# The products and sums of a feed-forward weight on GpSimd instead of VectorE, with newly planned engine orders, in a transformer layer on eight cores

## The chip, the cores and the metric

One Trainium2 chip (trn2), eight cores, one program on all of them; each core computes one of the eight batch elements. The time is the device time in microseconds of the slowest core. The engines of a core are TensorE (PE in the rows, PEld for its weight loads), VectorE (DVE), ScalarE (ACT), GpSimd (POOL) and SyncE (SP). Each executes its own instructions in a fixed order and waits on semaphores; transfers run beside them.

## The reference

For each batch element x is 2048 x 1024 in fp32, with 16 heads of width 64:

```python
x = x + attention(layernorm(x)) @ Wo + bo      # Q, K, V from Wq, Wk, Wv; scores / 8 + mask; softmax
# mask(i, j): -inf for j > i, 0 for j == i, -0.25 * log(i - j) for j < i
x = x + ffn(layernorm(x))
# ffn: complex product of the halves of x with W_real, W_imag (512 x 512 each), plus bias
W = einsum('abcd,cefg->abefdg', G1, G2).reshape(512, 512)     # c = 4 terms; once real, once imaginary
```

So each of the two feed-forward matrices is a sum of four outer products of small factors, and the kernel needs them as one 1024 x 1024 bf16 weight (real, imaginary, and minus imaginary, each where it belongs).

## The kernel before

**Stages.** The queries come in four chunks (c) of 512 rows. Each has 8 pairs of heads (p), and for each pair the keys come in tiles of 128 (mt, 4c + 4 of them). One (c, p, mt) is a step; there are 320, numbered g. A step is: two score matmuls on TensorE into stP (lines 1118 and 1120), an exp on ScalarE over both heads into PT (line 996), a product with the decay factors on VectorE (line 857), and twelve matmuls of 32 columns width for pv and for the denominators pr (lines 1142 and 1148). After a pair's last step ScalarE takes the reciprocal of pr by Ln and Exp (1004, 1006) and VectorE writes attnT (874).

Between the steps TensorE runs groups, each a matmul chain into one of two banks gp: T (transposes of the normalised xnrot, line 1044), K, Q (1057), V (1067), N and B (norm bounds for the exp's bias, 1078 and 1083), O (output projection, 1093), F (feed-forward, 1103). Each group is evicted by VectorE or ScalarE; some evictions of K, Q and T go to whichever the planner picks.

**The feed-forward weight.** It is built in 8 units (real and imaginary, four row tiles each) of 7 steps: a product of broadcast slices of g1s and g2s into wacc, then three times a product into wtmp and a sum wacc + wtmp. All are 128 x 512 fp32 (`wf_step`, lines 785 to 807, on VectorE). Each step waits for the one before by the semaphore s_wf. After step 7 of a unit ScalarE rounds wacc into two places of Wf (`wf_round`, lines 971 to 978); the next unit's first step waits for both by s_wfr. The factors g1s and g2s are the last transfers of GpSimd's first batch (lines 653 and 655). All eight units have to be done before attnT of chunk 2 is written (line 863, since wacc lies in its memory), before V of the last tile and before the first F group.

**What sets the order.** `make_fill` deals the groups out between the steps; this isn't touched. `make_orders` then lists all work as tasks with an engine, a length in us and predecessors, and simulates the engines: on ScalarE and VectorE it takes, of the tasks that are ready, the one with the earliest latest time. Its result, ACT_ORDER, DVE_ORDER and PE_ORDER, is emitted as it stands. Key lines of it are the tasks of the exp ("X", line 280), of the decay product ("P", 282), of the weight steps ("W", 316) and of the roundings ("WR", 318), and the lag after each task (lines 338 and 409):

```python
task("act", ("X", g), 0.19 + 0.00088 * w, ("S", g), ...)
task("dve", ("P", g), 0.03 + 0.00063 * w, ("X", g), ...)
task("dve", ("W", i), 0.6, ("W", i - 1) if i else ("dma", "g"), ...)
```

GpSimd's own program is short: an iota, the first batch of loads, then from line 659 on a wait for the last K group, the load of Wo, and the transfers that add bo and bfn.

Of the kernel before, what the change touches and what calls it, by code (L numbers as in the profile page):

```python
# [29 lines left out]
PATIENCE = (0.1, 0.15, 0.2, 0.3)  # L30
ROUNDS = 4
# [184 lines left out]
def make_orders(plan):  # L216
# [21 lines left out]
    for k in pe:  # L238
# [8 lines left out]
        else:  # L247
# [9 lines left out]
            if k1 == PASSES[what]:  # L257
# [41 lines left out]
    for i, (c, p) in enumerate(pairs):  # L299
        n = c * 4 + p // 2 - 2  # L300
        task("dve", ("SQ", c, p), 0.75, ("E", ("K", c, p)), ("E", ("Q", c, p)), i and ("SQ",) + pairs[i - 1],
             n >= 0 and ("D", ("N", n // 4, n % 4)))
    for c in range(NCH):
        for h in range(2):
            before = (c, 0) if h else (c - 1, 1) if c else None
            task("dve", ("BD", c, h), 0.15, ("E", ("N", c, 2 * h)), ("E", ("N", c, 2 * h + 1)), before and ("BL",) + before)
            task("act", ("BL", c, h), 0.3, ("BD", c, h), c and ("D", ("B", c - 1, h)))
            task("dve", ("BM", c, h), 0.12, ("BL", c, h), before and ("BM",) + before, c and ("D", ("B", c - 1, h)))
            task("dve", ("BN", c, h), 0.15, ("E", ("B", c, h)), before and ("BN",) + before)
# [17 lines left out]
    def latest(pe_at):  # L327

        late = {}
        for k in tasks:  # L330
            stack = [] if k in pe_at or k in late else [k]
            while stack:
# [4 lines left out]
                else:  # L337
                    late[k] = min([pe_at.get(u, late.get(u)) for u in users[k]] + [1e4]) - tasks[k][1] - 0.12
# [890 lines left out]
```

## Time and profile before

| | us |
|---|---|
| median of 3 runs | 563.18 (561.47 to 565.92) |
| the profiled execution | 561.32 |
| its span, slowest core (7) | 559.8 |
| spans of the eight cores | 555.4 to 559.8 |
| TensorE busy | 517.1 |
| VectorE busy | 461.3 |
| ScalarE busy | 381.9 |
| GpSimd busy | 38.3 |

The span runs from the first to the last instruction of a core, and the time holds what lies around it besides. Busy time is the sum over an engine's instructions; matmuls are pipelined, so a busy TensorE isn't one at its peak. In rows of groups, what stands behind the first bar is busy time in us and the mean of one in ns, and behind the second bar the idle time of the engine just before them with what ended it. A stretch A:B is in us from the span's start.

### The profile page before, as it was taken

Reading aid. Unit: us, or ns where it says so; the run is one execution under the profiler, and the core shown is the slowest. Engines: PE = TensorE matmul, PEld = TensorE weight load, DVE = VectorE, ACT = ScalarE, POOL = GpSimd, SP = SyncE. Lnnn points to the kernel's source line nnn. Section 1 sums busy time; section 2 is a strip of 40 time slices with the busy share of each in tenths; the row PEclk is TensorE's granted clock in tenths of the full one; section 3 lists DMA queues with packets and bytes.
Section 4 is the critical chain, followed back from the end, with each engine's and each line's share of the span. In section 5 each row is a group of like instructions: output and inputs, shape, how many; then the busy total and the mean of one; then the engine's idle time right before and its main releaser. Section 6 shows DMA issues by size and latency. Waiting matters only on the chain.

```text
span 559.8 us, 16753 instructions; the slowest of 8 cores (555.4 to 559.8 us)
## 1 busy us (share of the span) xinstructions
PE 517.1 (92%) x6096; PEld 241.2 (43%) x6096; DVE 461.3 (82%) x830; ACT 381.9 (68%) x526; POOL 38.3 (7%) x51
## 2 busy tenths in 40 slices
PE   1798989899999999989999999999999999999986
PEld 1334444344443444444444444444545444444442
DVE  5645999999999999887777887887888888888683
ACT  3425776778888879866767777777778777786010
POOL 7000000000000000000000020201101011111110
PEclk9999999999999999989999999999999999999999
DMA  8999231000120000010000089756566666457574
GB/s 200 187 170 253 78 114 39 3 2 2 40 78 2 8 34 1 2 47 33 1 3 2 1 121 185 150 137 148 135 152 152 152 151 141 97 130 171 146 153 150
DMA packets 16479, 52.77 MB, mean 94 GB/s; under 512 B 2000, under 2 KB 2000, under 8 KB 15632
## 3 DMA queue, kind: packets, MB, share of 16 engines
q0 software_dynamic: 7328, 28.05, 27.5%
q1 hardware_dynamic: 9072, 23.65, 12.7%
q8 instruction: 52, 0.85, 0.7%
q14 instruction: 27, 0.22, 0.1%
HBM read 51.69 MB, written 8.39 MB: 107 GB/s over the span
## 4 chain that ended last, share of the span: by engine, by line
PE 69%; DVE 9%; ACT 8%; issue 7%; DMA 5%; DVEq 0%; ACTq 0%; POOLq 0%
PE gp L1057 18%; PE stP L1118 11%; PE pv L1142 10%; PE gp L1093 8%; PE gp L1067 8%; PE gp L1103 8%; ACT PT L996 5%; PE pr L1148 4%; DMA Wo<-wo 3%; PE gp L1044 2%; DMA x<-bfn 1%; DVE stat L700 1%; DVE x L773 1%; DVE V L748 1%; DVE attnT L874 1%
## 5 line engine op out<-in xcount | busy, mean ns | idle before, releaser
L996 ACT ACTIVATE PT<-stP,negc 128x1024 bf16<-128x1024 f32 (+1 forms) x320 | 301.4, 983 | 81.8 <-PE stP L1120 80.1
L857 DVE TENSOR_TENSOR PT<-PT,decay 128x1024 bf16<-128x1024 bf16 (+1 forms) x320 | 190.7, 603 | 35.0 <-ACT PT L996 33.2
L1142 PE MATMUL pv<-PT,V 128*32 128x256 bf16 (+3 forms) x2560 | 101.4, 258 | 1.5 <-DVE PT L857 0.5
L1118 PE MATMUL stP<-QT,KT 64*128 64x512 bf16 (+1 forms) x320 | 94.5, 350 | 5.2 <-ACT PT L996 5.0
L1120 PE MATMUL stP<-QT,KT 64*128 64x512 bf16 (+1 forms) x320 | 95.1, 352 | 0.0
L1148 PE MATMUL pr<-PT,ones 128*32 128x256 bf16 (+3 forms) x1280 | 81.2, 257 | 0.7 <-issue 0.7
L1067 PE MATMUL gp<-Wv,xnT 128*128 128x512 bf16 x256 | 67.3, 385 | 8.6 <-DVE V L748 5.0
L1142 PEld LDWEIGHTS pv<-PT,V 128*32 128x32 bf16 x2560 | 56.7, 96 | 38.2 <-issue 35.9
L1057 PE MATMUL gp<-xnT,Wk 128*128 128x512 bf16 x256 | 66.7, 389 | 2.5 <-ACT xnT L968 2.0
L1057 PE MATMUL gp<-xnT,Wq 128*128 128x512 bf16 x256 | 65.0, 380 | 1.0 <-DVE KT L755 0.9
L1093 PE MATMUL gp<-Wo,attnT 128*128 128x512 bf16 x256 | 63.3, 380 | 2.4 <-DVE x L773 1.7
L1103 PE MATMUL gp<-Wf,xn2T 128*128 128x512 bf16 x256 | 63.6, 380 | 2.0 <-DVE outb L782 1.2
L1118 PEld LDWEIGHTS stP<-QT,KT 64*128 64x128 bf16 x320 | 22.6, 93 | 70.4 <-issue 67.3
L874 DVE TENSOR_TENSOR attnT<-pv,recip 64x512 bf16<-64x512 f32 x64 | 44.0, 687 | 4.8 <-ACT recip L1006 3.9
L1067 PEld LDWEIGHTS gp<-Wv,xnT 128*128 128x128 bf16 x256 | 21.6, 99 | 38.5 <-issue 20.7
L1103 PEld LDWEIGHTS gp<-Wf,xn2T 128*128 128x128 bf16 x256 | 22.8, 97 | 34.0 <-issue 11.4
L1057 PEld LDWEIGHTS gp<-xnT,Wq 128*128 128x128 bf16 x256 | 23.1, 98 | 32.3 <-issue 8.7
L1057 PEld LDWEIGHTS gp<-xnT,Wk 128*128 128x128 bf16 x256 | 22.6, 99 | 33.2 <-issue 12.6
L1093 PEld LDWEIGHTS gp<-Wo,attnT 128*128 128x128 bf16 x256 | 22.0, 97 | 34.4 <-issue 13.8
L1044 PE MATMUL gp<-ident_s,xnrot 128*128 128x128 bf16 x256 | 23.3, 233 | 14.3 <-DVE xnrot L710 13.7
L1148 PEld LDWEIGHTS pr<-PT,ones 128*32 128x32 bf16 x1280 | 34.6, 97 | 1.3 <-issue 0.8
L782 DVE TENSOR_TENSOR outb<-gp,x 128x512 f32<-128x512 f32 x32 | 22.1, 690 | 9.9 <-PE gp L1103 9.3
(71 smaller groups left out, 432.1 us busy)
## 6 DMA issues: line engine op xcount, KB each, us to landing
xrot<-x SPq DMA_DIRECT2D x21, 512.0 KB, 4.5
x<-bfn POOLq DMA_DIRECT2D x16, 512.0 KB, 6.4
out<-outb SPq DMA_DIRECT2D x32, 256.0 KB, 3.3
xrot<-bo POOLq DMA_DIRECT2D x12, 512.0 KB, 5.8
xfirst<-x SPq DMA_DIRECT2D x4, 512.0 KB, 6.2
Wk<-wk POOLq DMA_DIRECT2D x2, 1024.0 KB, 21.3
Wq<-wq POOLq DMA_DIRECT2D x2, 1024.0 KB, 27.0
Wv<-wv POOLq DMA_DIRECT2D x2, 1024.0 KB, 32.6
```

The lines of the kernel that those rows point to most:

```text
L857: v.tensor_mul(pt, pt, decay[:, off + no:off + 512].unsqueeze(1).to_broadcast([128, 2, 512 - no])).then_inc(s_pm, 1)
L874: ins = v.tensor_mul(out, pv[x:x + 64, :].rearrange("p (d m q) -> p d m q", d=2, q=64), recip[x:x + 64, :].rearrange("p (m q) -> p m q", q ...
L996: a.activation(p_tile(g, no), st_tile(g, no), AF.Exp, bias=negc[:, c * 8 + p % 2 * 4 + p // 2:][:, 0:1]).then_inc(s_exp, 1)
L1044: ins = t.transpose(ps[:, :].bitcast(BF16)[:, k * 128:(k + 1) * 128], xnrot[:, o + k * 128:o + (k + 1) * 128], ident[:, 0:128])
L1057: ins = t.matmul(ps[:, :], W[:, o:o + 128], xnTv[:, k, :], start=(k == 0), stop=(k == FT - 1))
L1067: ins = t.matmul(ps[:, :], xnTv[:, k, j * 128:(j + 1) * 128], Wv[:, half * 4096 + k * 512:half * 4096 + (k + 1) * 512], start=(k == 0), st ...
L1093: ins = t.matmul(ps[:, :], attnT[:, o + k * 512:o + k * 512 + 128], Wo[:, k * D + ch * 512:k * D + (ch + 1) * 512], start=(k == 0), stop=( ...
L1103: ins = t.matmul(ps[:, :], xn2Tv[:, i % 2, k], Wf[:, k * D + ch * 512:k * D + (ch + 1) * 512], start=(k == 0), stop=(k == FT - 1))
L1118: t.matmul(stP[g % 2][:, no:512], KT[0:64, ks:ks + 128], QT[0:64, qs + no:qs + 512], start=True, stop=True, tile_position=(0, 0))
L1120: t.matmul(stP[g % 2][:, 512 + no:1024], KT[64:128, ks:ks + 128], QT[64:128, qs + no:qs + 512], start=True, stop=True, tile_position=(64, ...
L1142: t.matmul(pv[x:x + 32, half * 256 + no // 2:(half + 1) * 256], V[:, vo + h * 64 + half * 32:vo + h * 64 + half * 32 + 32], p_part(g, h, a ...
L1148: ins = t.matmul(pr[x:x + 32, no // 2:256], ones32[:, :], p_part(g, h, a, no), start=first, stop=last, tile_position=(0, x), skip_group_ch ...
```

## The change

The 56 steps of `wf_step` move word for word from VectorE's program to GpSimd's (the engine `v` becomes `g`). There they stand behind the loads of g1s and g2s and ahead of the wait for the last K group and the load of Wo. In the planner the steps become tasks of no engine with 1.3 us each; the lengths of most other tasks are set anew, mostly shorter, and the lag after a task is 0.18 instead of 0.12 us.

```diff
+LAG = 0.18
...
-                us = {"B": 0.3, "T": 0.65}.get(what, 0.67)
+                us = {"B": 0.25, "K": 0.67, "Q": 0.67}.get(what, 0.61)
...
-        task("act", ("X", g), 0.19 + 0.00088 * w, ("S", g), g and ("X", g - 1), g >= PR and ("V", g - PR),
+        task("act", ("X", g), 0.14 + 0.000853 * w, ("S", g), g and ("X", g - 1), g >= PR and ("V", g - PR),
...
-        task("dve", ("P", g), 0.03 + 0.00063 * w, ("X", g), ("P", g - 1) if g else ("M", 3))
+        task("dve", ("P", g), 0.068 + 0.00052 * w, ("X", g), ("P", g - 1) if g else ("M", 3))
...
-        task("dve", ("W", i), 0.6, ("W", i - 1) if i else ("dma", "g"), i >= 7 and i % 7 == 0 and ("WR", i // 7 - 1), i == 0 and ("M", 2))
+        task("dma", ("W", i), 1.3, ("W", i - 1) if i else ("dma", "g"), i >= 7 and i % 7 == 0 and ("WR", i // 7 - 1), i == 0 and ("M", 2))
         if i % 7 == 6:
-            task("act", ("WR", i // 7), 1.4, ("W", i))
+            task("act", ("WR", i // 7), 1.05, ("W", i))
...
-            finish(k, end + 0.12)
+            finish(k, end + LAG)
...
             g.dma_start(out=g2s[:, :].rearrange("p (t n) -> p t n", t=4),
                         in_=dg2.rearrange("(t p) n -> p t n", p=128)).then_inc(s_g, 16)
+
+            def wf_step(n):
+
+                u, k = divmod(n, 7)
...
+                if n == 0:
+                    g.wait_ge(s_g, 32)
+
+                    g.wait_ge(s_mask, 2)
+                else:
+                    g.wait_ge(s_wf, n)
+                if k == 0 and u >= 1:
+                    g.wait_ge(s_wfr, 2 * u)
...
+                    g.tensor_mul(acc3 if k == 0 else tmp3,
...
+                else:
+                    g.tensor_add(wacc[:, :], wacc[:, :], wtmp[:, :]).then_inc(s_wf, 1)
+
+            for n in range(56):
+                wf_step(n)
...
-                elif what == "W":
-                    wf_step(*n)
```

VectorE's order, from the first full-width decay product of the pair that begins with exp 20. Before (L857 decay product, L803 and L807 the weight's product and sum):

```order
L857 TENSOR_TENSOR PT<-PT,decay 128x1024
L803 TENSOR_TENSOR wtmp<-g1s,g2s 128x512
L874 TENSOR_TENSOR attnT<-pv,recip 64x8x64 x2
L764 TENSOR_SCALAR QT<-gp,bq_s 128x512
L857 TENSOR_TENSOR PT<-PT,decay 128x2x384
L820 TENSOR_TENSOR sqb<-QT 128x512
L821 TENSOR_TENSOR sqb<-KT 128x512
L857 TENSOR_TENSOR PT<-PT,decay 128x2x256
L807 TENSOR_TENSOR wacc<-wacc,wtmp 128x512
L693 BN_STATS stat<-xrot 128x6
L857 TENSOR_TENSOR PT<-PT,decay 128x2x128
L803 TENSOR_TENSOR wtmp<-g1s,g2s 128x512
```

VectorE's order at the same place, of the change (L862 is the decay product now, L784 an eviction of K):

```order
L862 TENSOR_TENSOR PT<-PT,decay 128x1024
L784 TENSOR_SCALAR KT<-gp,cols_s 128x512
L879 TENSOR_TENSOR attnT<-pv,recip 64x8x64 x2
L862 TENSOR_TENSOR PT<-PT,decay 128x2x384
L722 BN_STATS stat<-xrot 128x6
L825 TENSOR_TENSOR sqb<-QT 128x512
L826 TENSOR_TENSOR sqb<-KT 128x512
L729 BN_STATS stat<-xrot 128x6
L731 BN_AGGR stat<-stat 128x2
L862 TENSOR_TENSOR PT<-PT,decay 128x2x256
L862 TENSOR_TENSOR PT<-PT,decay 128x2x128
```

The weight's steps are gone from between the decay products; evictions and layer-norm statistics have closed up.

ScalarE's order around the first rounding, which before stands behind exp 29 (L996 exp, L976 and L978 rounding, L1004 and L1006 reciprocal):

```order
L996 ACTIVATE PT<-stP,negc 128x1024
L996 ACTIVATE PT<-stP,negc 128x2x384
L976 ACTIVATE Wf<-wacc 128x512
L978 ACTIVATE Wf<-wacc 128x512
L1004 ACTIVATE recip<-pr 128x256
L1006 ACTIVATE recip<-recip 128x256
```

ScalarE's order around the first and second rounding of the change, behind exp 15 and behind exp 18 (L999 exp, L979 and L981 rounding):

```order
L999 ACTIVATE PT<-stP,negc 128x2x128
L979 ACTIVATE Wf<-wacc 128x512
L981 ACTIVATE Wf<-wacc 128x512
L988 ACTIVATE nrmx<-nrmx,cst 128x2
L961 ACTIVATE bexp<-gp,cst 128x8
L971 ACTIVATE xnT<-gp 128x8x128
L999 ACTIVATE PT<-stP,negc 128x1024
...
L999 ACTIVATE PT<-stP,negc 128x2x256
L979 ACTIVATE Wf<-wacc 128x512
L981 ACTIVATE Wf<-wacc 128x512
L999 ACTIVATE PT<-stP,negc 128x2x128
```

The eight roundings stand behind exps 29, 40, 51, 66, 74, 87, 101 and 110 before, and behind exps 15, 18, 24, 31, 38, 45, 52 and 60 in the change.

GpSimd's order behind its first batch of loads, of the change; before, the load of Wo follows g2s directly:

```order
L655 DMA g1s<-g1t 128x4x256
L657 DMA g2s<-g2t 128x4x128
L678 TENSOR_TENSOR wacc<-g1s,g2s 128x512
L678 TENSOR_TENSOR wtmp<-g1s,g2s 128x512
L682 TENSOR_TENSOR wacc<-wacc,wtmp 128x512
L678 TENSOR_TENSOR wtmp<-g1s,g2s 128x512
...
L682 TENSOR_TENSOR wacc<-wacc,wtmp 128x512
L689 DMA Wo<-wo 128x8x1024
```

All 56 steps stand ahead of the load of Wo.

## Rows read from the trace of the kernel before

**Rows 1.** The page, busy time: us (share of the span) and instructions.

```profile
PE 517.1 (92%) x6096; PEld 241.2 (43%) x6096; DVE 461.3 (82%) x830; ACT 381.9 (68%) x526; POOL 38.3 (7%) x51
```

**Rows 2.** Stretches: length, busy PE, PEld, DVE, ACT, POOL (instructions), clock, DMA share, GB/s.

```profile
80.00:100.00 20.00, 19.18 (x219) 8.82 (x212) 19.32 (x40) 14.96 (x27) 0.00 (x0) 1.00 0.17 54
100.00:120.00 20.00, 17.71 (x221) 7.91 (x221) 19.52 (x37) 14.41 (x24) 0.00 (x0) 1.00 0.01 3
120.00:150.00 30.00, 29.01 (x379) 13.49 (x371) 29.03 (x56) 24.02 (x37) 0.00 (x0) 1.00 0.06 20
150.00:226.00 76.00, 72.99 (x920) 32.81 (x919) 74.68 (x141) 65.14 (x92) 0.00 (x0) 1.00 0.08 23
...
240.00:320.00 80.00, 75.91 (x980) 35.25 (x972) 62.63 (x113) 57.46 (x69) 0.00 (x0) 0.98 0.05 15
320.00:500.00 180.00, 176.65 (x2323) 83.69 (x2321) 150.60 (x259) 138.87 (x173) 21.38 (x25) 1.00 0.64 142
```

**Rows 3.** Tiles wacc and wtmp: count, min/median/max ns, first and last start.

```profile
L807 DVE TENSOR_TENSOR wacc<-wacc,wtmp x24: 680/683/693, 96.4 to 223.1; 128x512 f32<-128x512 f32 x24
L803 DVE TENSOR_TENSOR wacc<-g1s,g2s x8: 674/682/691, 80.7 to 214.6; 128x512 f32<-128x512 f32 x8
L976 ACT ACTIVATE Wf<-wacc x8: 621/630/638, 105.8 to 225.2; 128x512 bf16<-128x512 f32 x8
L978 ACT ACTIVATE Wf<-wacc x8: 614/624/638, 106.3 to 225.7; 128x512 bf16<-128x512 f32 x8
...
L803 DVE TENSOR_TENSOR wtmp<-g1s,g2s x24: 680/682/693, 92.0 to 222.3; 128x512 f32<-128x512 f32 x24
```

**Rows 4.** Tile g2s: its load's issue on GpSimd, and the time to landing.

```profile
L655 POOL DMA_DIRECT2D g2s<-g2t x1: 767/767/767, 12.7 to 12.7; - x1
...
DMA to landing us min/median/max: 44.9/44.9/44.9
```

**Rows 5.** Groups of GpSimd: the iota.

```profile
L639 POOL IOTA B<- 128x2432 f32 x1 | 2.2, 2152 | 0.4 <-POOLq L436 0.4
```

**Rows 6.** The exps (line 996) from 0 to 80 us, and from 0 to 152 us.

```profile
L996 ACT ACTIVATE PT<-stP,negc x16: 468/790/1114, 43.8 to 77.1; 128x1024 bf16<-128x1024 f32 x4, 128x768 bf16<-128x768 f32 x4, 128x512 bf16<-128x512 f32 x4, 128x256 bf16<-128x256 f32 x4
...
L996 ACT ACTIVATE PT<-stP,negc x60: 464/901/1119, 43.8 to 151.5; 128x1024 bf16<-128x1024 f32 x27, 128x768 bf16<-128x768 f32 x11, 128x512 bf16<-128x512 f32 x11, 128x256 bf16<-128x256 f32 x11
```

**Rows 7.** Timeline, 5 to 17 us, xnrot and one DMA issue; then line 710, tile xrot.

```profile
7.63 0.91 DVE L710 TENSOR_SCALAR xnrot<-xfirst,stat 128x1024 bf16<-128x1024 f32 x1 [0.85 <-ACT stat L923]
...
11.51 0.86 DVE L710 TENSOR_SCALAR xnrot<-xfirst,stat 128x1024 bf16<-128x1024 f32 x1
...
12.66 0.77 POOL L655 DMA_DIRECT2D g2s<-g2t  x1
...
12.89 1.06 DVE L710 TENSOR_SCALAR xnrot<-xfirst,stat 128x1024 bf16<-128x1024 f32 x1
...
15.82 0.80 DVE L710 TENSOR_SCALAR xnrot<-xfirst,stat 128x1024 bf16<-128x1024 f32 x1
...
L710 DVE TENSOR_SCALAR xnrot<-xrot,stat x12: 803/806/809, 53.6 to 249.2; 128x1024 bf16<-128x1024 f32 x12
```

**Rows 8.** Line 857 in all, and GpSimd's transfers of bfn.

```profile
L857 DVE TENSOR_TENSOR PT<-PT,decay x320: 265/681/694, 45.0 to 518.1; 128x1024 bf16<-128x1024 bf16 x128, 128x512 bf16<-128x512 bf16 x32
...
L671 POOL DMA_DIRECT2D x<-bfn x16 | 13.6, 851 | 71.3 <-DVE xnrot L710 71.3
```

**Rows 9.** From 80 to 150 us: line 857 as a stretch, squares and xnrot as groups.

```profile
80.00:150.00 70.00, 22.24 (x41) 1.00 0.08 25
...
L820 DVE TENSOR_TENSOR sqb<-QT 128x512 bf16<-128x512 bf16 x8 | 3.4, 420 | 0.0
L821 DVE TENSOR_TENSOR sqb<-KT 128x512 bf16<-128x512 bf16 x8 | 3.3, 418 | 0.0
L710 DVE TENSOR_SCALAR xnrot<-xrot,stat 128x1024 bf16<-128x1024 f32 x2 | 1.6, 806 | 0.0
```

More of the change, by code:

```diff
@@ L300, in make_orders @@
         n = c * 4 + p // 2 - 2
-        task("dve", ("SQ", c, p), 0.75, ("E", ("K", c, p)), ("E", ("Q", c, p)), i and ("SQ",) + pairs[i - 1],
+        task("dve", ("SQ", c, p), 0.67, ("E", ("K", c, p)), ("E", ("Q", c, p)), i and ("SQ",) + pairs[i - 1],
              n >= 0 and ("D", ("N", n // 4, n % 4)))
@@ L305, in make_orders @@
             before = (c, 0) if h else (c - 1, 1) if c else None
[L306 to L309, printed above, removed]
+            task("dve", ("BD", c, h), 0.13, ("E", ("N", c, 2 * h)), ("E", ("N", c, 2 * h + 1)), before and ("BL",) + before)
+            task("act", ("BL", c, h), 0.19, ("BD", c, h), c and ("D", ("B", c - 1, h)))
+            task("dve", ("BM", c, h), 0.08, ("BL", c, h), before and ("BM",) + before, c and ("D", ("B", c - 1, h)))
+            task("dve", ("BN", c, h), 0.08, ("E", ("B", c, h)), before and ("BN",) + before)
     task("dve", ("M", 0), 2.8, ("A", 3))
@@ L337, in latest @@
                 else:
-                    late[k] = min([pe_at.get(u, late.get(u)) for u in users[k]] + [1e4]) - tasks[k][1] - 0.12
+                    late[k] = min([pe_at.get(u, late.get(u)) for u in users[k]] + [1e4]) - tasks[k][1] - LAG
                     stack.pop()
@@ L354, in length @@
         def length(k, engine):
-            return tasks[k][1] + (0.4 if engine == "act" and k[0] == "E" and k[1][0] == "T" else 0.0)
+            more = {"T": 0.31, "K": -0.08, "Q": -0.08}.get(k[1][0], 0.0) if engine == "act" and k[0] == "E" else 0.0
+            return tasks[k][1] + more
         def finish(k, t):
@@ L656, in _ @@
                         in_=dg2.rearrange("(t p) n -> p t n", p=128)).then_inc(s_g, 16)
+            def wf_step(n):
+                u, k = divmod(n, 7)
+                part, t = divmod(u, 4)
+                acc3 = wacc[:, :].rearrange("p (b e) -> p b e", b=32)
+                tmp3 = wtmp[:, :].rearrange("p (b e) -> p b e", b=32)
+                if n == 0:
[5 more added lines that the diff above has]
+                    g.wait_ge(s_wfr, 2 * u)
+                r = (k + 1) // 2
+                if k == 0 or k % 2 == 1:
+                    o1 = t * 256 + part * 128 + r * 32
+                    o2 = t * 128 + part * 64 + r * 16
+                    g.tensor_mul(acc3 if k == 0 else tmp3,
+                                 g1s[:, o1:o1 + 32].unsqueeze(2).to_broadcast([128, 32, 16]),
+                                 g2s[:, o2:o2 + 16].unsqueeze(1).to_broadcast([128, 32, 16])).then_inc(s_wf, 1)
+                else:
+                    g.tensor_add(wacc[:, :], wacc[:, :], wtmp[:, :]).then_inc(s_wf, 1)
+            for n in range(56):
+                wf_step(n)
             g.wait_ge(s_grp, GROUP_AT[("K", NCH - 1, PAIRS - 1)] + 1)
```

33 lines of the change are left out of this document (6 added, 27 removed).

## The prediction

> **What bounds the kernel now.** I read the page's table of busy time first, then the stretches. Over the whole span TensorE is busy 92%, VectorE 82%, ScalarE 68% and GpSimd 7% [rows 1], so TensorE looks like the only bound, and GpSimd like a free place to put work. The reader should not stop there: the table of stretches [rows 2] shows two regimes. From 80 to 226 us VectorE is busy 19.32 of 20, 19.52 of 20, 29.03 of 30 and 74.68 of 76 us, that is 98%, and TensorE 138.9 of 146 us, so it stands idle for 7.1 us (4.9%). From 320 to 500 us VectorE is at 84% and TensorE at 98.1%. So in the first stretch VectorE sets the pace, in the last one TensorE alone does.
>
> What the change takes off VectorE lies exactly in that first stretch: 24 sums of 0.683 us, 24 products into wtmp and 8 into wacc of 0.682 us, 56 steps from 80.7 to 223.8 us [rows 3]. That is 56 x 0.683 = 38.2 us of the engine that is full there. It looks like a gift. What it is worth depends on what GpSimd's version costs and whom it holds up.
>
> **Part 1, the steps leave VectorE.** If nothing came in their place, the stretch could not run better than TensorE allows. At the idle share of 320 to 500 us (1.9%) the 146 us would hold 2.8 us of TensorE idle instead of 7.1, a gain of 4.3 us; all idle gone would be 7.1 us. So the 38 us are worth 4 to 7 us at the most, because TensorE is next in line. I take 4.3.
>
> **Part 2, the chain on GpSimd.** The 56 steps wait for g2s, issued at 12.7 us and landed 44.9 us later [rows 4], so at 57.6 us; before, VectorE came to the first of them only at 80.7. In the old trace GpSimd runs no product or sum. Bounds from rows: the same operation on VectorE took 0.68 us [rows 3]; GpSimd's iota wrote 2,432 columns in 2.15 us [rows 5], 0.885 ns a column, and three passes over 512 columns (two reads and a write) would be an estimate of 1.36 us. The change's own planner puts 1.3 us for a step with its handshake. I take 1.3, near the upper end, since no GpSimd row here is faster per column than the iota. (The Trainium skill, GPSIMD Engine Reference, section 3.1, has a two-input sum of 2,048 fp32 columns at 4,497 ns; an estimate for 512 columns from it is 1.12 us, and no run here shows it yet.)
>
> Seven steps make a unit, then ScalarE rounds it twice (0.63 and 0.62 us, starts 0.5 us apart [rows 3], so 1.2 us with the handshake) before GpSimd may write wacc again: 7 x 1.3 + 1.2 = 10.3 us a unit. Now the order matters. ScalarE executes in a fixed order, and the new one puts the first rounding after exp 15 and the last behind exp 60, where they stood before after exp 29 and exp 110. By the old trace 16 exps had begun by 80 us, the last at 77.1, and 60 by 152 us, the last at 151.5 [rows 6]. From the first rounding (about 79 us) seven units follow: 79 + 7 x 10.3 = 151 us. The chain is as long as the stretch was before. So even with no side effect the stretch from 79 to 151 us gets no shorter than now: a faster VectorE would bring ScalarE earlier to a rounding whose sum isn't there, and behind that rounding wait the exps, and behind those the products with decay and TensorE's pv matmuls. The start has slack (first unit done at 57.6 + 9.1 = 67, wanted at 79), the seven others have none. What remains of part 1's gain is then the share after 151 us, 76 of 146 us: at most 3.0 us of TensorE idle [rows 2]. I take 2.
>
> **Part 3, what the two engines do to each other.** This has no price in the old trace, and the sum hangs on it. The nearest rows: VectorE's xnrot operation took 0.806 us in 12 of 12 cases when GpSimd did nothing, but 0.91, 0.86 and 1.06 us in the three cases that lay beside GpSimd's DMA issues, and 0.80 us once these had ended [rows 7]. So GpSimd can stretch a VectorE operation by 0.05 to 0.25 us even while it only issues transfers. Against it: the product with decay never took over 0.694 us in 320 cases, though GpSimd issued bias transfers beside it, 16 of bfn alone [rows 8]. So which operations collide matters, and the steps now moved read two tensors and write one, which no GpSimd instruction of the old trace does.
>
> From 80 to 150 us the VectorE operations that have two SBUF inputs, or that were seen to stretch, are 41 products with decay, 16 squares and 2 xnrot: 22.2 + 3.4 + 3.3 + 1.6 = 30.5 us in 59 instructions [rows 9]. Low end: no collision, 0 (a gain is excluded here, since part 1 has counted it). Middle: 59 x 0.13 us (mean of 0.10, 0.05 and 0.25) = 7.9 us, less than the 23 x 0.683 = 15.7 us of steps that leave VectorE in the same stretch, so it would vanish. High end: full exclusion, one waits whenever the other runs. Then the chain and these 30.5 us share one line; into the chain's pauses fit 7 x 1.2 us of roundings and 49 x 0.18 us of handshakes (the planner's figure), 17.2 us. The chain grows by 30.5 - 17.2 = 13.3 us if the pauses are used well, by 30.5 if not at all. The same from VectorE's side: a step that holds it for part of 1.3 us instead of 0.683 us of its own work gives nothing back. I take 15, near the lower end of exclusion: the traffic of a step is far heavier than that of a DMA issue, which already stretched operations by up to 0.25 us.
>
> The rule for it: the Trainium skill, SBUF — State Buffer, section "SBUF: two separate sides", says that VectorE and GpSimd share one read and write port pair by an exclusive lock, held for a whole instruction, by VectorE in a two-port mode or with two SBUF inputs (the latter only against a GpSimd operation that reads SBUF). By that rule the stretched xnrot and the unstretched decay product agree with the trace, and the moved steps are of the kind that blocks; it would give the 13 to 31 us above, and its absence 0. No row before shows the read case itself.
>
> **Part 4, the new orders elsewhere.** The planner is fed shorter lengths (a full exp 1.01 instead of 1.09 us, a full product 0.60 instead of 0.68) and more lag. The stretches' contents are the same, only their interleaving differs. Evictions on ScalarE fall from 50 to 44, on an engine that isn't the bound. From 226 us on there is little TensorE idle to win: 4.1 us in 240 to 320, 3.4 in 320 to 500 [rows 2]. Ends -3 to +3, taken as 0. Wo's load now stands behind the chain on GpSimd; it isn't due before about 320 us, when the chain has long ended, so it costs nothing unless the chain doubles.
>
> **Sum.** Execution profiled: 561.3 us (span 559.8). Part 3 +15, late relief -2, order 0: 574.3 us. The median of the three runs is 1.9 us higher (563.2), and single runs spread over 4.5 us, so I say 574.
>
> **Rivals.** (B) Faster: no collision worth the name. Place: 80 to 226 us, VectorE loses its 98%. For it: the decay product's steady 0.68 us beside DMA issues. Against it: the stretched xnrot, and a chain without slack. It gives 561.3 - 4.3 = 557, or 555 with a little from the orders; own range 551 to 560. It decides if a step stays at or under 1.2 us, so that the chain is no longer than the stretch.
> (C) No change: stretches of the middle kind, 7.9 us, are paid by the 15.7 us that left, and the chain paces as before: 562, own range 558 to 566.
> (D) Slower by the chain alone, with VectorE unharmed: if a step takes 1.6 us, each unit is 2.1 us late, and ScalarE waits 7 x 2.1 = 15 us at its roundings: 576. For it: the roundings stand where the plan had them just ready. Against it: the estimate from the iota ends at 1.36.
>
> **How the numbers follow.** A measurement of this kernel tells about 1% from no change. My forecast (A, both engines collide, 567 to 584) gets 0.40, D 0.05, B 0.36, C 0.19. The time is that of the likeliest: 574. The range goes from B's middle to A's upper end, 554 to 583; A's own range stands above. Slower by over 1%: A and D and the edge of C, 0.46. Faster by over 1% (under about 557.5 against the median): some 0.6 of B, 0.23. Within 1%: 0.31.
>
> **What would show it.** Right: GpSimd's steps last 1.3 us and more, with single ones much longer; decay products between 60 and 160 us above 0.694 us, or idle gaps before them that no other engine explains; ScalarE waiting for wacc before Wf; the 60th exp near 165 us instead of 151.5; after the chain VectorE well under 98%. Wrong: decay products all at 0.68 us beside GpSimd's steps (then B or C); steps of about 1.1 us and TensorE idle under 3 us from 80 to 226 us (B); decay products undisturbed and yet a wait for wacc at each rounding (D). A gain or loss mainly after 240 us would say that part 4 was the cause and my account of the stretch beside the point.

## The result: 4.2% slower, and the profile after

The changed kernel takes 589.14 us (median of 5 runs) against 564.64 us for the kernel before beside it: ratio 1.042, 95% interval 1.038 to 1.046. The profiled execution took 585.04 us. Medians here and below are over all runs, while ratios and intervals leave out those in which the cores of a die ran at a lower clock (one of the five, 649.4 us). I had forecast slower, 574 us with 554 to 583 as the range: the sign was right, but the forecast loss of 11 us is less than half of the 24 us measured.

The page of the changed kernel, busy time, and in 40 slices of the span VectorE's busy tenths and TensorE's granted clock:

```profile
PE 509.9 (87%) x6010; PEld 243.2 (42%) x6096; DVE 461.0 (79%) x780; ACT 379.2 (65%) x520; POOL 108.2 (19%) x107
...
DVE  5545999888989787768787687888888888888693
...
PEclk9999898989998999998999999999999999999999
```

VectorE is busy for 461.0 us, as before (461.3, [rows 1]), though 56 operations (38 us) have left it and only six have come (780 against 830; ScalarE has six fewer, 520 against 526). That is the first thing to see: something filled the hole. GpSimd rose by 69.9 us. The clock dips in the 5th, 7th, 9th and 13th slice, where the old page has a 9 in each; the old page has one 8 too, in the 18th slice, as the new one in its 19th.

The tiles wacc and wtmp, their instructions and who waited (answering [rows 3]):

```profile
L682 POOL TENSOR_TENSOR wacc<-wacc,wtmp x24: 1260/1269/1720, 63.3 to 174.2; 128x512 f32<-128x512 f32 x24
L678 POOL TENSOR_TENSOR wacc<-g1s,g2s x8: 1052/1054/1402, 60.9 to 165.8; 128x512 f32<-128x512 f32 x8
L979 ACT ACTIVATE Wf<-wacc x8: 620/628/638, 84.0 to 180.0; 128x512 bf16<-128x512 f32 x8
...
  ACT Wf L981: 38.4, 7
...
  POOL wacc L678: 38.4, 7
  ACT Wf L979: 0.3, 1
...
L678 POOL TENSOR_TENSOR wtmp<-g1s,g2s x24: 1052/1096/1495, 62.1 to 172.7; 128x512 f32<-128x512 f32 x24
```

A sum takes 1.27 us and a product 1.05 to 1.10, against 0.68 us on VectorE. GpSimd waited 38.4 us in seven cases for ScalarE's roundings, ScalarE only 0.3 us for GpSimd. So the chain of steps was next to never what ScalarE waited for.

VectorE's groups from 60 to 180 us, the kernel before first (the columns: busy us, mean ns, idle before):

```profile
L857 DVE TENSOR_TENSOR PT<-PT,decay 128x1024 bf16<-128x1024 bf16 x36 | 24.6, 682 | 0.3 <-ACT PT L996 0.2
L710 DVE TENSOR_SCALAR xnrot<-xrot,stat 128x1024 bf16<-128x1024 f32 x8 | 6.4, 806 | 0.0
L857 DVE TENSOR_TENSOR PT<-PT,decay 128x768 bf16<-128x768 bf16 x11 | 6.0, 550 | 0.1
...
L821 DVE TENSOR_TENSOR sqb<-KT 128x512 bf16<-128x512 bf16 x12 | 5.0, 418 | 0.0
L857 DVE TENSOR_TENSOR PT<-PT,decay 128x512 bf16<-128x512 bf16 x12 | 5.0, 415 | 0.0
L857 DVE TENSOR_TENSOR PT<-PT,decay 128x256 bf16<-128x256 bf16 x12 | 3.3, 277 | 0.0
```

The same groups of the changed kernel:

```profile
L862 DVE TENSOR_TENSOR PT<-PT,decay 128x1024 bf16<-128x1024 bf16 x25 | 21.6, 875 | 2.7 <-ACT PT L999 2.6
...
L739 DVE TENSOR_SCALAR xnrot<-xrot,stat 128x1024 bf16<-128x1024 f32 x8 | 9.1, 1136 | 0.0
L826 DVE TENSOR_TENSOR sqb<-KT 128x512 bf16<-128x512 bf16 x10 | 8.9, 888 | 0.0
L862 DVE TENSOR_TENSOR PT<-PT,decay 128x256 bf16<-128x256 bf16 x10 | 8.4, 844 | 1.0 <-ACT PT L999 1.0
L777 DVE TENSOR_TENSOR V<-gp,bvB 128x512 bf16<-128x512 f32 x11 | 7.6, 690 | 1.0 <-PE gp L1070 0.7
L825 DVE TENSOR_TENSOR sqb<-QT 128x512 bf16<-128x512 bf16 x10 | 7.5, 748 | 1.7 <-ACT QT L955 1.7
L862 DVE TENSOR_TENSOR PT<-PT,decay 128x768 bf16<-128x768 bf16 x9 | 6.8, 757 | 0.7 <-ACT PT L999 0.7
L862 DVE TENSOR_TENSOR PT<-PT,decay 128x512 bf16<-128x512 bf16 x10 | 6.4, 644 | 0.4 <-ACT PT L999 0.4
L722 DVE BATCH_NORM_STATS2 stat<-xrot 128x6 f32<-128x512 f32 x8 | 5.5, 683 | 0.0
```

The decay product of 256 columns went from 277 to 844 ns, that of 1024 columns only from 682 to 875: what is added doesn't grow with the operation's size, so it is a wait inside the operation's record and not a slower transfer of data. Operations with one input from PSUM (V) or a single 512-column SBUF input (bn_stats) keep their 0.69 us. Summed over the groups that grew: 25 x 0.193 + 9 x 0.207 + 10 x 0.229 + 10 x 0.567 + 10 x 0.470 + 10 x 0.328 + 8 x 0.330 = 25.3 us. These groups have 82 instructions, but not all of them grew. The row of line 862 in the same stretch has its median at 693 ns, the old length of a full product, and its longest at 1,754 ns, so some products wait long and many not at all:

```profile
L862 DVE TENSOR_TENSOR PT<-PT,decay x54: 275/693/1754, 65.1 to 179.7; 128x1024 bf16<-128x1024 bf16 x25, 128x512 bf16<-128x512 bf16 x10, 128x256 bf16<-128x256 bf16 x10, 128x768 bf16<-128x768 bf16 x9
```

The stretches from 60 to 180 us of the changed kernel (columns as in [rows 2]):

```profile
60.00:80.00 20.00, 14.58 (x156) 6.49 (x156) 19.53 (x30) 10.19 (x19) 8.29 (x7) 0.91 0.17 58
80.00:100.00 20.00, 16.46 (x146) 7.61 (x146) 18.94 (x32) 13.19 (x28) 9.59 (x8) 0.91 0.22 65
100.00:120.00 20.00, 15.78 (x216) 7.26 (x215) 18.01 (x30) 13.81 (x25) 13.73 (x13) 1.00 0.04 17
120.00:140.00 20.00, 16.86 (x192) 7.55 (x195) 15.80 (x25) 13.42 (x21) 12.86 (x11) 0.91 0.01 2
140.00:160.00 20.00, 15.52 (x182) 6.33 (x173) 19.15 (x22) 12.55 (x18) 15.97 (x13) 0.94 0.00 1
160.00:180.00 20.00, 16.92 (x182) 8.29 (x185) 18.17 (x27) 13.39 (x20) 9.10 (x7) 0.89 0.16 54
```

TensorE is idle for 120 - 96.1 = 23.9 us of these 120. This is core 2, whose trace lacks 86 of the 6,096 matmul records (x6010 on the page), and a missing record looks like idle time. The old trace's core 7 has them all and shows 7.1 us idle, so the fair comparison is with the old trace's core 2, which lacks 87 records:

```profile
60.00:180.00 120.00, 109.55 (x1371) 52.47 (x1388) 116.94 (x225) 94.46 (x150) 0.00 (x0) 1.00 0.12 38
```

There it is 120 - 109.55 = 10.5 us, so 13.4 us more in the change. The granted clock was 1.00 from 60 to 180 us before; a value of 0.91 means that the clock was at its lower level, 1.2 GHz, for 18% of the time, which takes 9% of the columns that could have passed. Summed, (0.09 + 0.09 + 0.09 + 0.06 + 0.11) x 20 = 8.8 us. Together 22.2 us are gone by 180 us. This only says where the time lies, not what caused it.

The exps of the changed kernel from 0 to 178 us, cut as in [rows 6]:

```profile
L999 ACT ACTIVATE PT<-stP,negc x60: 462/900/1115, 44.7 to 175.3; 128x1024 bf16<-128x1024 f32 x27, 128x768 bf16<-128x768 f32 x11, 128x512 bf16<-128x512 f32 x11, 128x256 bf16<-128x256 f32 x11
```

The 60th exp begins at 175.3 us instead of 151.5, 23.8 us late, and the spans differ by 583.5 - 559.8 = 23.7 us. These are the slowest cores, 2 against 7; on core 2 of both traces the exp is 22.8 us late (152.5 before). The loss arises while GpSimd's steps run; what comes behind them adds or wins back little.

### The profile page after: what moved, and what is told of

Its sections match the earlier page's. It is cut to its first block, busy times and chain, and to the rows that moved or that the text cites. A ratio compares the mean times of both kernels' runs of the same rounds, so it can differ in the third digit from the quotient of the medians.

```text
span 583.5 us, 16667 instructions; the slowest of 8 cores (578.7 to 583.5 us)
## 1 busy us (share of the span) xinstructions
PE 509.9 (87%) x6010; PEld 243.2 (42%) x6096; DVE 461.0 (79%) x780; ACT 379.2 (65%) x520; POOL 108.2 (19%) x107
## 4 chain that ended last, share of the span: by engine, by line
PE 55%; DVE 19%; issue 12%; ACT 9%; DMA 4%; DVEq 1%; ACTq 0%; another core or an unknown queue 0%; POOLq 0%
PE gp L1060 14%; PE stP L1121 8%; PE gp L1096 7%; PE pv L1145 7%; ACT PT L999 6%; PE gp L1070 6%; PE gp L1106 6%; DVE PT L862 4%; DMA Wo<-wo 3%; PE pr L1151 3%; DVE attnT L879 2%; DVE stat L729 2%; DVE xnrot L739 2%; PE gp L1047 2%; DVE stat L722 2%
## 5 line engine op out<-in xcount | busy, mean ns | idle before, releaser
L999 ACT ACTIVATE PT<-stP,negc 128x1024 bf16<-128x1024 f32 (+1 forms) x320 | 301.0, 981 | 89.8 <-PE stP L1123 86.7
L862 DVE TENSOR_TENSOR PT<-PT,decay 128x1024 bf16<-128x1024 bf16 (+1 forms) x320 | 204.5, 651 | 58.6 <-ACT PT L999 56.6
L1070 PE MATMUL gp<-Wv,xnT 128*128 128x512 bf16 x232 | 64.4, 401 | 14.4 <-DVE V L777 5.3
L1060 PE MATMUL gp<-xnT,Wk 128*128 128x512 bf16 x239 | 64.5, 398 | 6.0 <-issue 1.8
L1096 PE MATMUL gp<-Wo,attnT 128*128 128x512 bf16 x237 | 59.0, 380 | 7.8 <-DVE x L802 2.1
L1060 PE MATMUL gp<-xnT,Wq 128*128 128x512 bf16 x247 | 63.0, 385 | 2.7 <-DVE KT L784 1.7
L1106 PE MATMUL gp<-Wf,xn2T 128*128 128x512 bf16 x239 | 59.4, 380 | 4.2 <-issue 2.1
L1121 PEld LDWEIGHTS stP<-QT,KT 64*128 64x128 bf16 x320 | 22.2, 94 | 70.1 <-issue 67.4
L1047 PE MATMUL gp<-ident_s,xnrot 128*128 128x128 bf16 x256 | 23.8, 235 | 16.5 <-DVE xnrot L739 13.9
L682 POOL TENSOR_TENSOR wacc<-wacc,wtmp 128x512 f32<-128x512 f32 x24 | 32.7, 1361 | 3.4
```

Source lines behind the costliest of these rows:

```text
L862: v.tensor_mul(pt, pt, decay[:, off + no:off + 512].unsqueeze(1).to_broadcast([128, 2, 512 - no])).then_inc(s_pm, 1)
L999: a.activation(p_tile(g, no), st_tile(g, no), AF.Exp, bias=negc[:, c * 8 + p % 2 * 4 + p // 2:][:, 0:1]).then_inc(s_exp, 1)
L1047: ins = t.transpose(ps[:, :].bitcast(BF16)[:, k * 128:(k + 1) * 128], xnrot[:, o + k * 128:o + (k + 1) * 128], ident[:, 0:128])
L1060: ins = t.matmul(ps[:, :], W[:, o:o + 128], xnTv[:, k, :], start=(k == 0), stop=(k == FT - 1))
L1070: ins = t.matmul(ps[:, :], xnTv[:, k, j * 128:(j + 1) * 128], Wv[:, half * 4096 + k * 512:half * 4096 + (k + 1) * 512], start=(k == 0), st ...
L1096: ins = t.matmul(ps[:, :], attnT[:, o + k * 512:o + k * 512 + 128], Wo[:, k * D + ch * 512:k * D + (ch + 1) * 512], start=(k == 0), stop=( ...
```

## The experiments

All ratios are against the kernel before, run beside the experiment.

### One part at a time

**move_only**: the steps in GpSimd's program (added lines), with all orders of the kernel before.

```diff
+            for n in range(56):
+                wf_step(n)
...
-                elif what == "W":
-                    wf_step(*n)
```

> The 56 steps go to GpSimd as in the change, but every order (VectorE's without the steps, ScalarE's, TensorE's) stays that of the kernel before, so the roundings stand behind exps 29 to 110. Theory 1 (GpSimd's steps hold up VectorE's operations with two SBUF inputs): nearly the whole loss stays, ratio 1.03 to 1.045 against the kernel before; VectorE's decay products between 60 and 180 us have durations up to 1.7 us. Theory 2 (the newly planned orders lose the time, by the early roundings or otherwise): ratio 0.99 to 1.01. Theory 3 (a chain that ScalarE waits for at its roundings): the roundings come late here, so at most 1.01.

Measured: 590.08 us, ratio 1.0447 (1.0394 to 1.0501). Moving the steps alone gives the whole loss, as theory 1 had it; the new orders aren't needed for it. The early roundings aren't either, since they stand behind exps 29 to 110 here.

**plan_only**: the new planner numbers, the steps on VectorE.

```diff
-        task("dma", ("W", i), 1.3, ("W", i - 1) if i else ("dma", "g"), ...
+        task("dve", ("W", i), 0.61, ("W", i - 1) if i else ("dma", "g"), ...
```

> The planner has the new lengths and the lag of 0.18, but the 56 steps stay on VectorE (0.61 us each in the plan). Theory 1 (collision): nothing of the loss, ratio 0.99 to 1.005. Theory 2 (new orders): most of the loss, ratio over 1.02.

Measured: 571.11 us, ratio 1.014 (1.007 to 1.021). A miss for both: the new orders cost 1.4% of their own when VectorE still has the steps.

**no_steps**: the change's orders, no products or sums anywhere.

```diff
+                if k == 6:
+                    w = 16 if u else 512
+                    g.iota(wacc[:, 0:w], [[1, w]], base=n, channel_multiplier=1,
+                           allow_small_or_imprecise_dtypes=True).then_inc(s_wf, 1)
```

> The change's orders, but GpSimd computes no products and sums at all: one tiny iota per unit lets ScalarE round. Left out: the contents of the feed-forward weight. It shows what VectorE's relief alone is worth. Theory 1: faster than the kernel before by the 4 us of my part 1, ratio 0.985 to 0.998, TensorE's granted clock back at 0.99 or more. Theory 2 (orders): ratio 1.02 or more, since the orders are those of the change.

Measured: 563.4 us, ratio 0.9997 (0.9961 to 1.0033). With 38 us of VectorE's work gone and no price paid for it, the kernel is as fast as before; the gain that theory 1 expected (0.985 to 0.998) isn't there. By 180 us of the profile 78 exps had begun in both. So the relief was worth nothing with these orders.

**no_steps_old**: the same omission with the orders of the kernel before. The lines are those of no_steps, put into move_only:

```diff
-                g.wait_ge(s_wf, n)
...
+                if k == 6:
+                    w = 16 if u else 512
```

> The orders of the kernel before, with the 56 steps left out on every engine (one tiny iota per unit on GpSimd releases the roundings). Left out: the contents of the feed-forward weight. It gives what VectorE's relief is worth with the old orders, against 0.9997 with the new ones. If the newly planned orders cost something of their own (1.014 with the steps on VectorE): ratio 0.985 to 0.995 here. If the relief is worth nothing whatever the order, since TensorE is next in line: 0.997 to 1.003.

Measured: 562.66 us, ratio 0.9938 (0.9903 to 0.9972), 3.5 us. This is the most that another place for the steps can bring with the old orders. The new orders cost some 0.6% against the old ones here (the two intervals just overlap), and nothing that can be told between the change (1.042) and move_only (1.0447). Why it doesn't show there wasn't tested.

### What in GpSimd's step collides

**write_only**: each step is two iotas, which write wacc and wtmp and read nothing.

```diff
+                g.iota(wacc[:, :], [[1, 512]], base=n, channel_multiplier=1, ...)
+                g.iota(wtmp[:, :], [[1, 512]], base=n, channel_multiplier=1, ...).then_inc(s_wf, 1)
```

> The change's orders and its chain, but each of the 56 steps is two iotas of 512 columns on GpSimd, some 1 us together, which write SBUF and read nothing. Left out: the contents of the feed-forward weight. Theory 1a (the collision is about reading: GpSimd must read SBUF to block operations with two SBUF inputs): decay products and squares keep 0.68 and 0.42 us, only xnrot is stretched, ratio 0.985 to 1.005. Theory 1b (any GpSimd instruction blocks them): decay products stretched as in the change, ratio 1.02 or more. Theory 3 (length of the chain): close to the change, since the chain is nearly as long.

Measured: 565.49 us, ratio 1.0012 (0.9981 to 1.0043). GpSimd was busy 61.4 us from 60 to 180 us, and VectorE's groups in that stretch of write_only read:

```profile
L855 DVE TENSOR_TENSOR PT<-PT,decay 128x1024 bf16<-128x1024 bf16 x36 | 24.3, 684 | 8.6 <-ACT PT L992 8.6
L732 DVE TENSOR_SCALAR xnrot<-xrot,stat 128x1024 bf16<-128x1024 f32 x9 | 7.4, 822 | 0.0
...
L855 DVE TENSOR_TENSOR PT<-PT,decay 128x256 bf16<-128x256 bf16 x12 | 3.4, 285 | 1.0 <-ACT PT L992 1.0
```

The decay products are untouched, xnrot's operation is longer by 2%. Writing alone costs this kernel no time, nor does a chain of this kind ahead of the roundings. It isn't free of collisions, as the probe below shows for xnrot's operation.

**copy_only**: each step is two copies of 512 columns, one SBUF input each.

```diff
+                g.tensor_copy(wacc[:, :], g1s[:, 0:512])
+                g.tensor_copy(wtmp[:, :], g1s[:, 512:1024]).then_inc(s_wf, 1)
```

> The change's orders and chain, each of the 56 steps being two copies of 512 fp32 columns on GpSimd: one SBUF input instead of two. Left out: the contents of the feed-forward weight. Theory 1a (any GpSimd instruction that reads SBUF blocks VectorE's two-input operations for as long as it lasts): decay products stretched, ratio 1.01 to 1.04, by the copies' total time. Rival 1c (only GpSimd's two-input instructions block): durations as in the kernel before, ratio 0.995 to 1.005.

Measured: 577.19 us, ratio 1.0227 (1.0162 to 1.0291). GpSimd's groups and two of VectorE's from 60 to 180 us:

```profile
L673 POOL COPY wtmp<-g1s 128x512 f32<-128x512 f32 x56 | 42.2, 753 | 0.0
L672 POOL COPY wacc<-g1s 128x512 f32<-128x512 f32 x56 | 39.6, 708 | 78.3 <-DMA g2s<-g2t 48.1 <-ACT Wf L972 23.6 <-POOL wtmp L673 0.4
...
L853 DVE TENSOR_TENSOR PT<-PT,decay 128x1024 bf16<-128x1024 bf16 x27 | 23.7, 888 | 4.3 <-ACT PT L990 4.2
...
L853 DVE TENSOR_TENSOR PT<-PT,decay 128x256 bf16<-128x256 bf16 x11 | 5.6, 509 | 0.9 <-ACT PT L990 0.9
```

Reading one input is enough. 81.8 us of copies cost half of what 69.6 us of products and sums cost (the 256-column product reaches 509 ns in the mean, not 844). By the same sum as above VectorE's operations grew by 16.0 us, and the kernel by 2.3% of 565.7, 12.8 us. Why a copy holds VectorE up for less than a sum was not tested: a copy is shorter, but it also reads one input instead of two.

**half**: units 0 to 3 on GpSimd (the first lines), 4 to 7 on VectorE (the last ones), old orders.

```diff
+            for n in range(28):
+                wf_step(n)
...
                 elif what == "W":
+                    if n[0] >= 28:
+                        wf_step(*n)
```

> The orders of the kernel before; units 0 to 3 (28 steps) on GpSimd, units 4 to 7 (28 steps) on VectorE. All 56 on GpSimd with these orders gave 1.045. Theory 1 (each step costs its own collision): 1.018 to 1.027. Rival (a fixed cost, as TensorE's clock falling once GpSimd interferes at all, or the first stretch alone): 1.035 or more, or under 1.01.

Measured: 574.24 us, ratio 1.0144 (1.0084 to 1.0204). Half the steps, a third of the loss, and at the interval's upper end nearly half. This is below the 1.018 to 1.027 expected for a cost by the step, and the interval reaches under 1.01, where the rival stood. A fixed cost of 3.5% or more is excluded; that the loss grows in proportion to the steps isn't shown.

**probe**: no layer, twenty VectorE operations per phase with GpSimd beside them.

```diff
+        PHASES = [("P1024", None), ("P1024", "add"), ("P256", "add"), ("sq", "add"), ("bn", "add"), ("xn", "add"),
+                  ("psum", "add"), ("P1024", "copy"), ("P1024", "iota"), ("xn", "iota"), (None, "add"), (None, "copy")]
```

> Nothing of the layer is computed; the output is left meaningless. Twenty VectorE operations per phase, alone or beside a chain of GpSimd instructions: the decay product of 1024 columns alone; then beside 16 sums (512 fp32) the decay product of 1024 and of 256 columns, a square, a bn_stats (one SBUF input), xnrot's operation (one fp32 input), and a sum from PSUM; then the decay product beside 28 copies and 28 iotas, xnrot's beside iotas; then sums and copies alone. Theory 1: beside sums the decay product, the square and xnrot's operation reach 1.3 us and more in single cases, bn_stats and the sum from PSUM keep 0.68; beside iotas the decay product keeps 0.68. Sums alone take 1.26 us, as the shortest in the change. Rival (the stretching is a matter of bandwidth, shared by all operations): every VectorE operation is longer by the same share beside sums, bn_stats too, and none reaches the length of a sum on top of its own.

VectorE's timeline of probe (start us, length us of the twenty together, instruction), in the order of the phases, the last two left out (they have no VectorE operation):

```profile
9.07 15.81 DVE L142 TENSOR_TENSOR PT<-PT,decay 128x1024 bf16<-128x1024 bf16 x20 [0.17 <-DVE stat L131]
...
25.51 29.81 DVE L142 TENSOR_TENSOR PT<-PT,decay 128x1024 bf16<-128x1024 bf16 x20 [0.43 <-issue]
...
55.52 23.80 DVE L142 TENSOR_TENSOR PT<-PT,decay 128x256 bf16<-128x256 bf16 x20
...
79.53 24.47 DVE L145 TENSOR_TENSOR sqb<-QT 128x512 bf16<-128x512 bf16 x20
...
104.56 15.85 DVE L148 BATCH_NORM_STATS2 stat<-xrot 128x6 f32<-128x512 f32 x20
...
127.67 30.24 DVE L151 TENSOR_SCALAR xnrot<-xrot,stat 128x1024 bf16<-128x1024 f32 x20
...
158.12 15.81 DVE L155 TENSOR_TENSOR V<-gp,bvB 128x512 bf16<-128x512 f32 x20
...
181.86 19.95 DVE L142 TENSOR_TENSOR PT<-PT,decay 128x1024 bf16<-128x1024 bf16 x20
...
208.77 15.82 DVE L142 TENSOR_TENSOR PT<-PT,decay 128x1024 bf16<-128x1024 bf16 x20
...
228.89 19.97 DVE L151 TENSOR_SCALAR xnrot<-xrot,stat 128x1024 bf16<-128x1024 f32 x20
```

GpSimd's side as groups: sums beside the decay product of 1024 columns and alone, copies beside it and alone, iotas beside it and beside xnrot's operation:

```profile
L102 POOL TENSOR_TENSOR wacc<-wacc,wtmp 128x512 f32<-128x512 f32 x16 | 24.1, 1509 | 24.8 <-DVE cst L161 22.7
...
L102 POOL TENSOR_TENSOR wacc<-wacc,wtmp 128x512 f32<-128x512 f32 x16 | 20.2, 1260 | 2.6 <-DVE cst L161 0.5
...
L104 POOL COPY wacc<-g1s 128x512 f32<-128x512 f32 x28 | 22.7, 809 | 4.3 <-DVE cst L161 0.8
...
L104 POOL COPY wacc<-g1s 128x512 f32<-128x512 f32 x28 | 17.2, 613 | 4.0 <-DVE cst L161 0.5
...
L106 POOL IOTA wacc<- 128x512 f32 x28 | 15.6, 557 | 4.2 <-DVE cst L161 0.5 <-POOL wacc L106 0.4
...
L106 POOL IOTA wacc<- 128x512 f32 x28 | 22.3, 795 | 3.9 <-DVE cst L161 0.5
```

Twenty decay products take 15.81 us alone, 29.81 us beside 16 sums (14.0 us more, 0.88 us a sum), 19.95 us beside 28 copies and 15.82 us beside 28 iotas. bn_stats and the sum from PSUM keep 15.8 us beside the same sums: it isn't bandwidth shared by all. Beside GpSimd's sums and copies the waits fall on chosen VectorE operations only: those with two SBUF inputs, and xnrot's with one fp32 input of 1024 columns. Beside GpSimd's iotas, which only write, the decay product keeps its length, but xnrot's operation does not escape: it took 0.896 us in the mean (0.806 in the kernel before), and the iotas went from 0.557 to 0.795 us, 6.7 us in all.

Who pays differs. Beside the decay product of 1024 columns the 16 sums lose 3.9 us and VectorE 14.0; the 28 copies lose 5.5 us and VectorE 4.1; beside xnrot's operation the iotas lose 6.7 us and VectorE some 1.8 (20 x 0.09).

### How far VectorE's lost time explains the loss

**emulate**: no steps, but 48 extra bn_stats on VectorE in the stretch.

```diff
+                if 13 <= g <= 60:
+                    o = (g - 13) * 6
+                    v.bn_stats(wtmp[:, o:o + 6], bvB[:, 0:512])
```

> The kernel without steps (new orders, the contents of the feed-forward weight left out; 0.9997 of the kernel before), with 48 extra bn_stats of 512 columns on VectorE, one ahead of each decay product of the steps 13 to 60, 0.61 us each from start to start: 29 us, about the 27 us by which VectorE's operations were longer beside GpSimd's steps between 60 and 180 us. No GpSimd step runs. Theory (the loss is VectorE's lost time in this stretch, and what TensorE's clock adds once TensorE waits): ratio 1.03 to 1.045 and a mean clock of 0.98 to 0.99, as in the change. Rival (something else of the collision costs, as GpSimd's own waits, or ScalarE's): under 1.02 with the clock at 0.995 or more.

Measured: 581.65 us, ratio 1.0303 (1.0274 to 1.0332), mean clock 0.993 over the cores and runs. 29 us of plain VectorE time cost 17 us. The ratio is just inside the theory's range, the clock above its 0.98 to 0.99. The profiled execution allows a comparison that bears on the clock: from 60 to 180 us core 0 had it at 0.96, core 3 at 1.00, and both traces have all records. Core 0, then core 3:

```profile
60.00:180.00 120.00, 101.73 (x1178) 46.45 (x1177) 115.09 (x223) 82.42 (x138) 1.01 (x7) 0.96 0.11 38
...
60.00:180.00 120.00, 98.29 (x1183) 45.35 (x1180) 116.26 (x225) 82.81 (x139) 1.56 (x8) 1.00 0.13 38
```

The 60th exp began at 167.0 us on core 0 and 167.7 on core 3, and the spans were 573.7 and 575.3 us. The core at full clock was not ahead; its TensorE was idle for 21.7 us where the other's was for 18.3. So the loss in emulate is there without the low clock.

**lumps**: the same 48, in pairs ahead of every second decay product.

```diff
-                if 13 <= g <= 60:
+                if 13 <= g <= 60 and g % 2:
...
+                    v.bn_stats(wtmp[:, o + 6:o + 12], bvB[:, 0:512])
```

> As emulate (no steps on any engine, 48 extra bn_stats on VectorE, 29 us), but in lumps: two of them, 1.22 us, ahead of every second decay product of the steps 13 to 60. The change's collisions are lumps of this length: a decay product of 256 columns beside a step took 0.84 us in the mean instead of 0.28. Emulate gave 1.030 with a mean clock of 0.993; the change 1.042 with 0.984. If the unevenness of the stalls makes the difference: 1.037 or more and a clock under 0.99. If not: 1.025 to 1.033 with a clock near 0.993, and the remaining 7 us belong to something that only GpSimd's real steps bring.

Measured: 585.7 us, ratio 1.0354 (1.0311 to 1.0397), clock 0.984 to 0.994 by core. Between the two expectations: the lumps cost 3 us more than the even load, but the intervals overlap, and so do those of lumps and the change (1.038 to 1.046). That unevenness makes the difference is suggested, not shown, and four us to the change's 1.042 stay without an experiment.

**fill_after** and its control **fill_none**: zero-weight matmuls ahead of the waits for decay products, to keep TensorE's clock up (the loop stands there twice).

```diff
+                if 8 <= g <= 64 and not first:
+                    for x in (0, 32, 64, 96):
+                        t.matmul(pr[x:x + 32, 128:256], zeros32[:, :], ident[:, 0:128],
+                                 start=False, stop=False, tile_position=(0, x), skip_group_check=True)
...
```

> The change with filler on TensorE: before each wait for a decay product of the steps 8 to 64 that aren't a pair's first, eight matmuls of 128 columns with zero weights accumulate nothing into pr. Question: does TensorE's granted clock, 0.89 to 0.94 in five of the stretches from 60 to 180 us of the change, carry a share of the loss of its own? Across cores and runs of the change a span is 0.55 us longer for each 0.001 of mean clock, which would put 9 of the 24 us on the clock. If so and if the filler keeps the clock up: clock above 0.99, 3 to 8 us faster than the change relative to what the filler costs in its control. Rival (the low clock only accompanies the stalls, TensorE having little to do there): clock up or not, no gain against the control's cost.

> Control: the same filler in the kernel without steps (new orders, the contents of the feed-forward weight left out), which took 0.9997 of the kernel before. It gives the filler's own cost: 49 steps x about 0.11 to 0.4 us, so 1.00 to 1.03.

Measured: fill_after 591.18 us, 1.0451 (1.0379 to 1.0523), control 568.44 us, 1.0063 (1.0022 to 1.0103). The mean clock over the cores was 0.986 against the change's 0.984: the filler didn't keep the clock up, so the pair doesn't decide what the clock is worth. The control cost 0.6%, inside its expectation.

**g_early**: an attempt at a faster kernel, g1s and g2s loaded behind the first half of Wv, the steps on VectorE.

```diff
             weight(Wv, dwv, 0, s_w["wv_a"])
+            g.dma_start(out=g1s[:, :]..., in_=dg1...).then_inc(s_g, 16)
+            g.dma_start(out=g2s[:, :]..., in_=dg2...).then_inc(s_g, 16)
```

> An attempt at a faster kernel: the steps stay on VectorE, but g1s and g2s are loaded behind the first half of Wv instead of last (the planner is told 38 us instead of 62, and 3 us more for the loads behind), so that VectorE can take steps from about 40 us on, where it is busy 58%. If VectorE's load from 80 to 226 us costs anything: 0.99 to 1.0, at best the 0.6% that leaving out all steps gave. If the later weights bind the start: 1.00 to 1.01.

Measured: 565.94 us, ratio 1.0027 (0.9992 to 1.0062). No gain. After no_steps_old this is no surprise: 0.6% was the most to be had. From 40 to 60 us TensorE was busy 14.7 us here and 18.5 in the kernel before, which fits the rival, the later weights, but isn't traced to them. No version that computes the weight beat the kernel before.

## Why the prediction was right in its sign and wrong in its size

**Right: the relief is small.** Part 1 put 4.3 us (7.1 at the very most) on 38 us of VectorE's time, because TensorE is next. no_steps_old gained 3.5 us and no_steps nothing. The late relief of 2 us in the sum was about 0: the 60th exp was 23.8 us late and the end 23.7.

**Right: what collides.** Part 3 named the operations with two SBUF inputs and xnrot's; those are the ones that grew, and V's evictions and bn_stats didn't. The Trainium skill's rule (SBUF — State Buffer, "SBUF: two separate sides") agrees with the rows of the two-input operations: the lock concerns VectorE's two-input operations only against a GpSimd operation that reads SBUF, and the decay products beside iotas kept 0.68 us. The evidence that I took from the old trace was real but narrow: xnrot's operation does collide with GpSimd instructions that only write (0.896 us beside the probe's iotas, 0.822 in write_only), and this says nothing of the decay product, which doesn't.

**Wrong: the account of the chain.** Parts 2 and 3 let the chain pace the stretch, "the seven others have none" (slack), and so priced the collision by how much the chain grows. The step's length was about right (1.3 us forecast; 1.05 to 1.27 us and some 0.14 us between them). But GpSimd waited 38.4 us for ScalarE, and ScalarE 0.3 us for it; rival D falls with that, and move_only, with late roundings, loses as much. So of the signs that I had named, ScalarE waiting for wacc failed, while the long single steps (up to 1.72 us), the decay products above 0.694 us and VectorE well under 98% behind the chain (87% from 180 to 200 us) came. The one who pays is VectorE. GpSimd's steps took 69.6 us in all, 5.7 us more than 24 x 1.26 + 32 x 1.05 = 63.9 us of their shortest forms; VectorE's operations grew by 25.3 us. The probe shows the same for sums beside the decay product: 3.9 us against 14.0.

**The step that failed: the +15 us of part 3.** It priced the collision as growth of GpSimd's chain, let 17.2 us of the chain's pauses hide more than half of the 30.5 us of colliding operations, and stayed near the lower end of 13 to 31. The pauses were longer than that (38.4 us of waiting), the chain held up next to nobody, and yet VectorE's operations grew by 25.3 us and the kernel by 24. The full exclusion worked out there, 31 us, was the nearer bound. How lost VectorE time turns into lost kernel time isn't one number: 29 us of it cost 17 us spread evenly (emulate) and 20 us in pairs (lumps), and per us by which VectorE's operations grew the kernel lost 0.94 us in the change, 0.80 in copy_only and 0.76 in move_only (25.2 us for 33.3, summed in the same way from 60 to 250 us). What makes the change the dearest of these stays open.

**The clock, for which the sum had no term.** In the account of 60 to 180 us it can stand for up to 8.8 us of the change. Over 32 core spans of four runs the mean clock is 0.984 and a span is 0.55 us longer for each 0.001 less of it (correlation -0.71); carried on to the old clock of 0.999 this gives 573 us, 8 of the 23 us between the mean spans of 581 and 558. But this is a correlation. Part of it comes from behind the steps: cores 2, 3, 5 and 6 of the profiled execution have a clock of 0.97 from 240 to 300 us and spans of 581.3 to 583.5 us, the others 1.00 and 578.7 to 580.5. And in emulate the low clock of core 0 cost nothing against core 3: it took the place of idle time, with VectorE busy for 115 to 116 of the 120 us on both. The filler failed to raise the clock. So the clock's share in the change lies between 0 and some 9 us and stays open, and a term for it was not what the forecast lacked in the first place.

**Part 4**, the new orders, was taken as 0 within 3 us. They cost about 0.6% without steps and 1.4% with the steps on VectorE, and didn't show between the change and move_only.

**Chances.** Case A had 0.40, its own range 567 to 584; the 589 lies above it. The full exclusion that I had worked out (31 us) gives 561.3 + 31 - 2 = 590 us and should have set the range's upper end, as the bound of an unknown cost.

## What to carry to other kernels

Before work goes to an idle engine, ask which instructions of the busy engine it blocks while it runs, and count those, not the hand-over of time: here GpSimd's 69.6 us of reading instructions added 25.3 us to VectorE's two-input operations and xnrot's, and its iotas, which only write, added next to nothing. Ask first what the relief is worth by leaving the work out altogether: 0.6% at best here, so there was hardly a price low enough. And when a cost has no row behind it, let its worked-out bound set the end of the range.

## What the runs showed of the hardware that I hadn't expected

- Who pays in the exclusion depends on the pair. Beside each other, 16 GpSimd sums lost 3.9 us and 20 decay products 14.0 us, but 28 GpSimd copies lost 5.5 us and the same products 4.1 us. A 256-column product that takes 277 ns alone took 844 ns in the mean between 60 and 180 us.
- The wait is in the VectorE operation's recorded length, not in idle time before it, so the engine looks as busy as before (461.0 against 461.3 us) with 56 operations fewer and six more.
- One SBUF input on GpSimd suffices: a copy of 512 fp32 columns took 0.61 us alone and held up decay products too, 4.1 us for 28 copies in the probe against 14.0 us for 16 sums.
- GpSimd's iotas, which only write, leave the decay product alone (15.82 against 15.81 us for twenty) but collide with xnrot's operation: 0.557 us an iota against 0.795.
- TensorE's granted clock fell in the change behind idle time, for one on core 2: from 65 to 70 us it was busy for 2.03 of 5 us, and from 70 to 75 us the clock was 0.77 of full speed. In emulate a core with such a fall (0.96 from 60 to 180 us) was no slower than one without, as idle time shrank instead.
